# A graph layer on one core: idle lanes of a gather read rows of their own in the second pass

## The chip, the core and the metric

The kernel runs on one core of one Trainium2 chip. The metric is the device time of one execution in microseconds; lower is better. The engines are PE (TensorE), DVE (VectorE), ACT (ScalarE), POOL (GpSimd) and SP (SyncE). SP's transfers go through queue q1 of the profile, POOL's gathers through queue q0.

## The reference

One graph layer over N = 8192 nodes with F = 256 features. The adjacency is dense in memory (8192 x 8192 floats) and sparse in content, with a weight that falls off as the inverse root of the row's number, so that early rows have many edges and late rows two on average.

```
h = relu(layernorm(x))
e = leaky_relu(h @ a[:F] + (h @ a[F:]).T, 0.2)
U = softmax(where(adj > 0, e, -9e15), axis=1)
rowsum = sum(0.5 * U * U, axis=1);  coe = sigmoid(temp)
prop_u = U @ h;  xi = h * rowsum
feat = shrink(coe[2] * (prop_u - xi) + (1 - coe[2]) * (h + prop_u - xi), 1e-6)
pu = U @ feat
odd = coe[0] * (feat - coe[3] * pu) + (1 - coe[0]) * h0
even = pu + (feat - coe[3] * pu) * rowsum
out = x + coe[1] * even + (1 - coe[1]) * odd
```

## The kernel before

The rows are cut into 64 tiles of 128; a row of a tile is a lane, one of the 128 partitions. The **first pass** streams the adjacency once, finds each row's edges, and keeps for tile t and lane p up to 16 column numbers (`IDX`), their softmax weights (`WGT`) and a tail (`JT`, `ROWE`, `WE`): once no more than 128 edges of a tile are left over, each of the 128 lanes of one last gather fetches one of them, and a small matrix sends it to its row. From these it makes `feat`, kept in HBM as `feat_d`, one row of 1 KB per node.

The **second pass** computes `U @ feat` for tiles 1 to 63. Tile t has D slots and a tail; slot k is one indirect DMA (`gather_slots`, L629 to L646) in which lane p fetches row `IDX[p, t, k]` of `feat_d`; the tail is one more (`gather_tail`, L648). Each fetches 128 rows. A lane that has no edge in a slot is idle: its number in the list is OUT = 2N = 16384. In the first pass the gathers have a bounds check and an idle lane fetches nothing. In the second pass there is none; there the list is first cut to N - 1 = 8191, so all idle lanes of a gather fetch the last row of `feat_d`. Its weight is zero, so the value doesn't matter.

PE multiplies each gathered tile by a diagonal matrix of weights (`DG`, made by ACT at L680) and sums in PSUM: `first_products` (L686) and `other_products` (L691), one `If` per slot, since D differs by tile. Tile 0 has been done densely; its blocks come through `pt_d` (L1688).

Buffers form a ring of RING = 4 tiles, and each engine runs its own loop over tiles with semaphores between:

- DVE: `stage(t)` waits until tile t-4 has been multiplied (`prod2_ready`), copies tile t's lists out of the large arrays into the ring slot (`RWR`, `IDR`, `IDT`, `WSR`; L1734 to L1737) and signals `staged`. Then `finish(t-3)` makes the output rows: L1744, L1745, a wait for the product, and L1752, which signals `out_made`.
- POOL: waits for `staged`, loads the number of slots, issues the slots' gathers and the tail's. For tiles 1 to 3 part of the gathers is issued ahead, at the end of the first pass (L903, with bounds check; the rest at L1661).
- SP: loads x, h0, feat and the block of `pt_d` of tile t (L1599 to L1602) once `out_made` of tile t-4 is there, and stores the output of tile t-3 (L1609).
- ACT: waits for `staged` and for the product of two tiles before, makes the diagonals.
- PE: waits for SP's loads, the diagonals, the gathers of the tile and `out_made` of tile t-2.

`Steps` (L253 and on) chains DVE instructions where one reads what the one before wrote: each signals a semaphore and the next waits for it.

Of the kernel before, what the change touches and what calls it, by code (L numbers as in the profile page):

```python
# [7 lines left out]
ALU = mybir.AluOpType  # L8
# [4 lines left out]
def adj_preln_kernel(nc, x, adj, h0, a, temp, out):  # L13
# [39 lines left out]
    with ctx:  # L53
# [132 lines left out]
        IDT = sb("IDT", [P, RING], i32)  # L186
        IDR = sb("IDR", [P, RING, KR], i32)
        WSR = sb("WSR", [P, RING, KR])
        M24 = sb("M24", [P, K])
        U = sb("U", [P, KR])  # L190
        JNKW = sb("JNKW", [P, K])
# [160 lines left out]
        def prepare_gpsimd(pool):  # L352
            nc.gpsimd.memset(zeros[:], 0.0)
            nc.gpsimd.memset(H[:, :, :, F + 2:AUG], 0.0).then_inc(tri_set, 1)
            nc.gpsimd.memset(R[:, HO + NH * GT * AUG:], 0.0)
            nc.gpsimd.memset(ONES_K[:], 1.0)
            nc.gpsimd.memset(SLOTW[:], 1.0)
            nc.gpsimd.memset(ABOVE[:], -2.0 ** -27)
            nc.gpsimd.iota(KB[:, 0], pattern=[[1, FW]], base=-FW // 2, channel_multiplier=0, allow_small_or_imprecise_dtypes=True)
            nc.gpsimd.memset(ONE_R[:], 1.0)  # L360
            nc.gpsimd.memset(ONESB[:], 1.0)
            nc.gpsimd.memset(ZB[:], 0.0)
            nc.gpsimd.memset(TRI[:], 1.0)
            nc.gpsimd.iota(IOTAE[:], pattern=[[1, P]], base=0, channel_multiplier=0, allow_small_or_imprecise_dtypes=True)
            nc.gpsimd.iota(IOTA1[:], pattern=[[1, P]], base=1, channel_multiplier=0, allow_small_or_imprecise_dtypes=True)
            nc.gpsimd.memset(kcc[:], 0.0)
            nc.gpsimd.memset(DOWN[:], -BIG)
            nc.gpsimd.memset(FLG[:, 0:1], 0.0)
            nc.gpsimd.memset(CTL[:, 0], 1)
            nc.gpsimd.memset(JT[:, 0:1], 0)  # L370
            nc.gpsimd.memset(ROWE[:, 0:1], 0.0)
            nc.gpsimd.memset(WE[:, 0:1], 0.0)
            nc.gpsimd.iota(NEGD[:], pattern=[[-1, KC]], base=1, channel_multiplier=0, allow_small_or_imprecise_dtypes=True)
            nc.gpsimd.iota(PIDX[:], pattern=[[0, 1]], base=0, channel_multiplier=1, allow_small_or_imprecise_dtypes=True)
            nc.gpsimd.iota(ED[:, K:K + 1], pattern=[[0, 1]], base=1, channel_multiplier=1, allow_small_or_imprecise_dtypes=True)
            nc.gpsimd.memset(PLACE[:], 0.0)
            for b in range(NB):
                nc.gpsimd.memset(DROP[:, b * FW // P:(b + 1) * FW // P], -2.0 ** (b + 1))
            nc.gpsimd.iota(OFFS[:].rearrange("one (g s) -> one g s", s=FW // P), pattern=[[0, NT * P // FW], [-P, FW // P]], base=FW - P, channel_multiplier=0).then_inc(tri_set, 1)
            pool.wait_ge(tri_set, 2)  # L380
            nc.gpsimd.memset(NEGD[:, 0:1], 2.0 ** 20)
            nc.gpsimd.memset(SLOTW[:, 0:1], 0.0)
            late = SLOTW[:, KP2 + 1:KC - 1].rearrange("p (a b) -> p a b", b=2)
            nc.gpsimd.memset(late[:, :, 0], 2.0)
            nc.gpsimd.memset(late[:, :, 1], 0.0)
            nc.gpsimd.memset(SLOTW[:, KC - 1:KC], float(2 - KC))
            nc.gpsimd.affine_select(out=TRI[:], in_=TRI[:], compare_op=ALU.is_gt, fill=0.0, base=0,
                                    pattern=[[1, P]], channel_multiplier=-1)
            nc.gpsimd.iota(back[:], pattern=[[-1, NT]], base=NT, channel_multiplier=0, allow_small_or_imprecise_dtypes=True)
            nc.gpsimd.memset(ident[:], 0.0).then_inc(ident_made, 1)  # L390
            pool.wait_ge(ident_made, 1)
            nc.gpsimd.affine_select(out=ident[:], in_=ident[:], compare_op=ALU.not_equal, fill=1.0, base=0,
                                    pattern=[[-1, P]], channel_multiplier=1).then_inc(ident_made, 1)
            for g in range(NG):
                u = g % NH
                pool.wait_ge(h_done[u], g // NH + 1)
                pool.dma_start(haug_g[g], H[:, u]).then_inc(h_stored[u], 16)
            for u in range(NH):
                pool.wait_ge(h_stored[u], 16 * uses(u))
# [1174 lines left out]
        diag2_ready = sem("diag2_ready")  # L1574
        prod2_ready = sem("prod2_ready")
        s4_step = sem("s4_step")
        out_made = sem("out_made")
        out_kept = [sem(f"out_kept{v}") for v in range(RING)]
        S0A, S1A = SELF, SELF2
# [141 lines left out]
        def second_vector(dve):  # L1721
            def coefs():
                step = Steps(dve, s4_step, 0, 5)
                nc.vector.memset(SW[:, 0:1], 0.0)
                step(nc.vector.tensor_scalar(S0A[:], ROWS[:], coe[:, 1:2], one_c0[:, 0:1], ALU.mult, ALU.add))
                step(nc.vector.tensor_scalar(S1A[:], S0A[:], coe[:, 3:4], -1.0, ALU.mult, ALU.mult))
                step(nc.vector.scalar_tensor_tensor(S1A[:], S1A[:], coe[:, 1:2], INVZ[:], ALU.add, ALU.mult))
                step(nc.vector.tensor_tensor(SW[:], S1A[:], SW[:], ALU.mult))
                step(nc.vector.tensor_tensor(S0A[:], S0A[:], SW[:], ALU.add))
                step.end()  # L1730

            def stage(t, v):
                dve.wait_ge(prod2_ready, t - 3 + RING)
                nc.vector.tensor_scalar(RWR[:, v], IOTA1[:], ROWE[:, bass.ds(t, 1)], WE[:, bass.ds(t, 1)], ALU.is_equal, ALU.mult)  # L1734
                nc.vector.tensor_scalar(IDR[:, v], IDX[:, bass.ds(t, 1)].rearrange("p a k -> p (a k)"), float(N - 1), None, ALU.min)
                nc.vector.tensor_scalar(IDT[:, v:v + 1], JT[:, bass.ds(t, 1)], float(N - 1), None, ALU.min)
                nc.vector.tensor_copy(WSR[:, v], WGT[:, bass.ds(t, 1)].rearrange("p a k -> p (a k)")).then_inc(staged, 1)  # L1737

            def finish(t, r, v):
                step = Steps(dve, s4_step, t * 2 + 5, 2)  # L1740
                first = isinstance(t, int) and t == 0
                part = TD if first else TR[:, v % 2]
                dve.wait_ge(t2_loaded[v], 64 * r + 64)
                step(nc.vector.scalar_tensor_tensor(part, FR[:, v], S0A[:, bass.ds(t, 1)], XR[:, v], ALU.mult, ALU.add))  # L1744
                step.mark(nc.vector.scalar_tensor_tensor(part, H0R[:, v], one_c0[:, 1:2], part, ALU.mult, ALU.add))  # L1745
                at_least(dve, out_kept[v], 16 * r)
                dve.wait_ge(prod2_ready, t + 1 + RING)
                step.need()
                if first:
                    dve.sem_inc(out_made, 1)  # L1750
                else:
                    nc.vector.scalar_tensor_tensor(OR[:, v], ACCS[v % 2], S1A[:, bass.ds(t, 1)], TR[:, v % 2], ALU.mult, ALU.add).then_inc(out_made, 1)  # L1752
                step.end()

            def body(t, r, v, live):
                if live(0):
                    stage(t, v)
                if isinstance(t, int) and t == 1:
                    coefs()
                if isinstance(t, int) and t == 3:  # L1760
                    each_dense(dve, dense)
                if live(3):
                    finish(*ring_earlier(t, r, v, 3))
            def dense(n):
                d = tile_of(dve, n)
                step = Steps(dve, e_step, n * 7, 7)
                nc.vector.tensor_copy(dsm[:, 3:4], INVZ[:, bass.ds(d, 1)])
                step(nc.vector.tensor_copy(dsm[:, 6:7], ROWS[:, bass.ds(d, 1)]))
                dve.wait_ge(own_loaded, 48 * n + 48)
                dve.wait_ge(acc2_ready, n + 1)  # L1770
                last = out_steps(step, ACC2, XD, FD, H0D, dsm[:, 3:4], dsm[:, 6:7], dsm[:, 8:10], T0[:], OD)
                last.then_inc(out_ready, 1)
                dve.wait_ge(out_ready, n + 1)
                dve.sem_inc(acc2_free, 1)
                step.end()
            dve.sem_inc(acc2_free, 1)
            dve.wait_ge(feat_made, NS)
            dve.sem_inc(out_made, RING)
            ring_turns(dve, body, 1, 3)
            dve.wait_ge(acc0_ready, 2)  # L1780
            nc.vector.scalar_tensor_tensor(OD0, ACC3, S1A[:, 0:1], TD, ALU.mult, ALU.add).then_inc(row0_made, 1)
# [56 lines left out]
```

## Time and profile before

| | us |
|---|---|
| median of 3 runs | 1517.84 |
| lowest, highest | 1516.83, 1520.83 |
| span of the profiled execution | 1535.4 |
| POOL busy in it | 589.9 (38%) |
| DVE busy | 931.9 (61%) |
| ACT busy | 863.7 (56%) |
| PE busy | 968.4 (63%) |

The profiled execution's only time is its span, 1535.4 us from the first to the last instruction; it is 17.6 us over the median of the unprofiled runs. The page draws the span in 40 slices of 38.4 us. The first pass fills slices 1 to 26: the DMA row stands at 9 and the rate at 350 to 390 GB/s. From slice 27 on (about 1000 us) the DMA row stands at 2 to 6, POOL at 5 and 6, DVE at 1 to 3. The loop of the second pass begins at about 1080 us, where the first gather of line 1661 stands.

### The profile page before, as it was taken

The page shows a single profiled execution, that of the slowest core. Times are in us where ns is not written, and L with a number is a line of the kernel's source. Part 1 is how long each engine was busy: PE and PEld are TensorE (multiplying, and loading weights), DVE is VectorE, ACT ScalarE, POOL GpSimd, SP SyncE. Part 2 cuts the span into 40 slices and gives each one's busy share as a digit, 9 for nine tenths or more (in the row PEclk, how much of TensorE's full clock was granted, in tenths as well). Part 3 has the DMA queues.
Part 4 walks back from the last instruction along what each step waited for, and adds up shares of the span by engine and source line. Part 5 has one row for each costly group of instructions (what it writes and reads, how often), then busy time and mean ns, then how long its engine had stood idle before and what let it go on. Part 6 is the DMA issues. An engine that isn't in the chain of part 4 may idle for free.

```text
span 1535.4 us, 27679 instructions
## 1 busy us (share of the span) xinstructions
PE 968.4 (63%) x3566; PEld 578.1 (38%) x3630; DVE 931.9 (61%) x5233; ACT 863.7 (56%) x1840; POOL 589.9 (38%) x649
## 2 busy tenths in 40 slices
PE   3545767776676767667777777753464564555656
PEld 3421345443333344334343333332343343333333
DVE  7756656667778788888888888875211122223333
ACT  4663777777788888888888888831221111111111
POOL 1004344443332233322222222245656565556553
PEclk9975687889899898897878788865677676767777
DMA  7989878889899999999999999822545455556665
GB/s 190 357 292 353 322 291 300 326 327 346 330 360 369 377 368 371 361 378 394 371 385 374 372 374 376 327 62 65 150 122 145 127 161 163 158 168 180 184 184 164
DMA packets 152837, 423.14 MB, mean 276 GB/s; under 512 B 31111, under 2 KB 114697, under 8 KB 136406
## 3 DMA queue, kind: packets, MB, share of 16 engines
q1 hardware_dynamic: 122492, 345.66, 61.0%
q0 software_dynamic: 30304, 77.05, 16.7%
q8 instruction: 11, 0.18, 0.0%
q14 instruction: 30, 0.25, 0.0%
HBM read 398.37 MB, written 33.90 MB: 282 GB/s over the span
## 4 chain that ended last, share of the span: by engine, by line
DVE 31%; issue 26%; PE 15%; SPq 11%; another core or an unknown queue 6%; ACT 4%; DMA 3%; DVEq 3%; ACTq 1%
PE TP L321 5%; PE ACC L693 2%; SPq L1599 2%; SPq L1609 2%; SPq L1602 2%; DVE XHO L1066 2%; PE ACC L689 2%; SPq L1601 2%; SPq L1600 2%; PE MISC L987 2%; DMA R<-in_x_dram 1%; ACT SG L309 1%; DVEq L257 1%; DVE JK L1133 1%
## 5 line engine op out<-in xcount | busy, mean ns | idle before, releaser
L309 ACT ACTIVATE SG<-W,ABOVE 128x4096 bf16<-128x4096 f32 x126 | 467.0, 3706 | 81.0 <-DVE cnt L1049 54.3
L634 POOL DMA_INDIRECT R<-haug_d,IDS x230 | 231.0, 1004 | 604.6 <-issue 591.1
L321 PE MATMUL TP<-SG,FOLD 128*128 128x512 bf16 x948 | 299.9, 458 | 4.4 <-issue 0.7
L680 ACT ACTIVATE DG<-ident,WSR 128x128 f32<-128x128 f32 x230 | 76.6, 392 | 373.5 <-remote 234.4
L1752 DVE SCALAR_TENSOR_TENSOR R<-ACC,SELF,R 128x256 f32<-128x256 f32 x63 | 30.5, 484 | 321.6 <-remote 238.3
L634 POOL DMA_INDIRECT W<-feat_d,IDR x140 | 133.9, 956 | 117.9 <-issue 117.9
L321 PEld LDWEIGHTS TP<-SG,FOLD 128*128 128x128 bf16 x1008 | 116.9, 125 | 118.8 <-issue 62.0
L689 PE MATMUL ACC<-R,DG 128*128 128x256 f32 x446 | 158.2, 502 | 2.8 <-issue 2.7
L688 PE MATMUL ACC<-XHO,ZB 128*128 128x256 bf16 x126 | 40.1, 318 | 179.6 <-ACTq L682 86.6
L689 PEld LDWEIGHTS ACC<-R,DG 128*128 128x128 f32 x446 | 100.3, 242 | 23.4 <-issue 6.8
L689 PE MATMUL ACC<-W,DG 128*128 128x256 f32 x274 | 98.9, 503 | 11.9 <-issue 11.9
L680 ACT ACTIVATE DG<-ident,WS 128x128 f32<-128x128 f32 x230 | 75.6, 391 | 29.8 <-issue 29.8
L688 PEld LDWEIGHTS ACC<-XHO,ZB 128*128 128x128 bf16 x126 | 12.6, 100 | 210.8 <-issue 132.5
L1688 PE MATMUL MISC<-R 128*128 128x256 f32 x128 | 51.6, 493 | 52.6 <-DMA R<-pt_d 40.8
L649 POOL DMA_INDIRECT R<-haug_d,IDT x63 | 63.0, 1001 | 37.7 <-issue 37.7
L689 PEld LDWEIGHTS ACC<-W,DG 128*128 128x128 f32 x274 | 61.9, 247 | 29.3 <-issue 19.4
L634 POOL DMA_INDIRECT R<-feat_d,IDR x52 | 49.7, 955 | 41.8 <-issue 41.8
L982 PE MATMUL MISC<-RC,ONESB 128*128 128x18 bf16 x61 | 11.7, 191 | 84.6 <-DVE RC L1181 84.4
L950 PE MATMUL OWNB<-HTS,R 128*128 128x256 f32 x116 | 39.4, 421 | 36.9 <-issue 19.6
L1688 PEld LDWEIGHTS MISC<-R 128*128 128x128 f32 x128 | 28.5, 242 | 69.0 <-DMA R<-pt_d 43.2
L803 ACT ACTIVATE WS<-SCR,msm 128x25 f32<-128x25 f32 x63 | 19.9, 316 | 60.6 <-DVE msm L1108 44.7
L649 POOL DMA_INDIRECT W<-feat_d,IDT x48 | 46.2, 962 | 16.3 <-issue 16.0
(295 smaller groups left out, 2292.7 us busy)
## 6 DMA issues: line engine op xcount, KB each, us to landing
W<-in_adj_dram SPq DMA_DIRECT2D x128, 2048.0 KB, 13.6
haug_d<-R POOLq DMA_DIRECT2D x8, 1056.0 KB, 9.7
HTS<-haug_d SPq DMA_DIRECT2D x64, 132.0 KB
R<-in_x_dram SPq DMA_DIRECT2D x8, 1024.0 KB, 6.6
R<-in_x_dram SPq DMA_DIRECT2D x64, 128.0 KB
R<-in_L_gnn_h_dram SPq DMA_DIRECT2D x64, 128.0 KB
R<-feat_d SPq DMA_DIRECT2D x64, 128.0 KB
out_dram<-R SPq DMA_DIRECT2D x64, 128.0 KB, 1.8
```

Of the source, the lines that this page charges most:

```text
L309: nc.scalar.activation(SG[:, u, half(h)], W2[:, u, half(h)], ACT.Sign, scale=2.0 ** 100, bias=ABOVE[:], accum_out=DEG[:, u, h:h + 1]).then ...
L321: nc.tensor.matmul(KP[u], FOLD[:, b], SG[:, u, b * FW:(b + 1) * FW], start=False, stop=False)
L634: pool.indirect_dma_start(out=g[:, k, 0:w], out_offset=None, in_=table, in_offset=bass.IndirectOffsetOnAxis(ap=ids[:, k:k + 1], axis=0), * ...
L649: pool.indirect_dma_start(out=g[:, KR, 0:w], out_offset=None, in_=table, in_offset=bass.IndirectOffsetOnAxis(ap=idt, axis=0), **limit).the ...
L680: nc.scalar.mul(DG[:, u, k], ident[:], weights[:, k:k + 1])
L688: nc.tensor.matmul(ACCS[u], ZB[:], COLS[:, 0:F], start=True, stop=False)
L689: first_slots(pe, slots, lambda k: nc.tensor.matmul(ACCS[u], DG[:, u, k], g[:, k, 0:F], start=False, stop=False))
L693: other_slots(pe, slots, lambda k: nc.tensor.matmul(ACCS[u], DG[:, u, k], g[:, k, 0:F], start=False, stop=False))
L950: nc.tensor.matmul(ACC0, PTB[:, w], HTS[:, uc, 0:F], start=False, stop=False)
L987: nc.tensor.matmul(SPR, RE[:, u], ED[:], start=True, stop=True).then_inc(spread, 1)
L1066: swap(KB[:, 0], FOUND[:, 0:8], KP[u], EMPTY).then_inc(keys_taken[u], 1)
L1688: own = nc.tensor.matmul(ACC3, PTR[:, v], FR[:, v], start=False, stop=False)
```

## The change

The change touches the second pass alone, but for one table that POOL writes in the prologue. An idle lane no longer gets the number N - 1, but one of its own: `AWAY[p, k] = 64 p + 3 k - OUT` is added to the list wherever it holds OUT, so that lane p reads row 64 p + 3 k in slot k (k = 16 for the tail). Rows have 1 KB: the lanes' idle rows lie 64 KB apart, the slots' 3 KB. All of them lie under row 8192.

```diff
+        AWAY = sb("AWAY", [P, KS1])
+        IDLE = sb("IDLE", [P, RING, KS1])
...
+            nc.gpsimd.iota(AWAY[:], pattern=[[3, KS1]], base=int(-OUT), channel_multiplier=N // P, allow_small_or_imprecise_dtypes=True)
...
+        idle_step = sem("idle_step")
...
             def stage(t, v):
                 dve.wait_ge(prod2_ready, t - 3 + RING)
                 nc.vector.tensor_scalar(RWR[:, v], IOTA1[:], ROWE[:, bass.ds(t, 1)], WE[:, bass.ds(t, 1)], ALU.is_equal, ALU.mult)
-                nc.vector.tensor_scalar(IDR[:, v], IDX[:, bass.ds(t, 1)].rearrange("p a k -> p (a k)"), float(N - 1), None, ALU.min)
-                nc.vector.tensor_scalar(IDT[:, v:v + 1], JT[:, bass.ds(t, 1)], float(N - 1), None, ALU.min)
+                step = Steps(dve, idle_step, t, 1)
+                ids = IDX[:, bass.ds(t, 1)].rearrange("p a k -> p (a k)")
+                nc.vector.scalar_tensor_tensor(IDLE[:, v, 0:KR], ids, float(N - 1), AWAY[:, 0:KR], ALU.is_gt, ALU.mult)
+                step(nc.vector.tensor_scalar(IDLE[:, v, KR:KS1], JT[:, bass.ds(t, 1)], float(N - 1), AWAY[:, KR:KS1], ALU.is_gt, ALU.mult))
+                step.end()
+                nc.vector.tensor_tensor(IDR[:, v], ids, IDLE[:, v, 0:KR], ALU.add)
+                nc.vector.tensor_tensor(IDT[:, v:v + 1], JT[:, bass.ds(t, 1)], IDLE[:, v, KR:KS1], ALU.add)
                 nc.vector.tensor_copy(WSR[:, v], WGT[:, bass.ds(t, 1)].rearrange("p a k -> p (a k)")).then_inc(staged, 1)
```

DVE's own order, one turn of the loop from the staging of a tile to the output before the next. Before (WI is the array that holds `IDX` and `WGT`, R the one with the ring's buffers):

```order
L1734 TENSOR_SCALAR R<-IOTA,ROWE,WE 128x128
L1735 ISA
L1735 TENSOR_SCALAR IDR<-WI 128x16
L1736 REGISTER_ALU
L1736 TENSOR_SCALAR IDT<-JT 128x1
L1737 ISA
L1737 COPY WSR<-WI 128x16
L1744 ISA
L1744 SCALAR_TENSOR_TENSOR R<-R,SELF 128x256
```

With the change, where L1753 is what was L1744:

```order
L1738 TENSOR_SCALAR R<-IOTA,ROWE,WE 128x128
L1741 ISA
L1741 SCALAR_TENSOR_TENSOR IDLE<-WI,AWAY 128x16
L1742 REGISTER_ALU
L1742 TENSOR_SCALAR IDLE<-JT,AWAY 128x1
L1744 TENSOR_TENSOR IDR<-WI,IDLE 128x16
L1745 TENSOR_TENSOR IDT<-JT,IDLE 128x1
L1746 ISA
L1746 COPY WSR<-WI 128x16
L1753 ISA
L1753 SCALAR_TENSOR_TENSOR R<-R,SELF 128x256
```

Two DVE instructions and one wait have come in ahead of the copy to `WSR`, which signals `staged`; the order of the rest, and of the gathers on POOL, is as it was.

## Rows read from the trace of the kernel before

**Rows 1.** Windows of the second pass: busy us of each engine, clock, DMA share, GB/s.

```profile
core 0: us, PE busy (x) PEld busy (x) DVE busy (x) ACT busy (x) POOL busy (x), PEclk, DMA share, GB/s
1100.00:1150.00 50.00, 27.77 (x93) 20.38 (x92) 7.59 (x28) 10.26 (x33) 28.42 (x31) 0.69 0.43 118
...
1450.00:1500.00 50.00, 27.50 (x82) 16.65 (x82) 17.88 (x68) 6.75 (x20) 25.97 (x28) 0.77 0.64 182
```

**Rows 2.** POOL's groups by line, 1030 us to the end.

```profile
L634 POOL DMA_INDIRECT W<-feat_d,IDR x140 | 133.9, 956 | 117.9 <-issue 117.9
L634 POOL DMA_INDIRECT R<-feat_d,IDR x52 | 49.7, 955 | 41.8 <-issue 41.8
L649 POOL DMA_INDIRECT W<-feat_d,IDT x48 | 46.2, 962 | 16.3 <-issue 16.0 <-DVE WSR L1737 0.3
```

**Rows 3.** POOL's timeline: four gathers, a long gap, the next two.

```profile
1246.18 0.95 POOL L634 DMA_INDIRECT W<-feat_d,IDR  x1 [0.31 <-issue]
1247.43 0.95 POOL L649 DMA_INDIRECT W<-feat_d,IDT  x1 [0.30 <-issue]
1254.29 0.95 POOL L634 DMA_INDIRECT W<-feat_d,IDR  x1 [5.91 <-issue]
1255.54 1.05 POOL L634 DMA_INDIRECT W<-feat_d,IDR  x1 [0.31 <-issue]
```

**Rows 4.** POOL's timeline: first and last of the 28 gaps over 0.6 us.

```profile
1121.18 0.95 POOL L634 DMA_INDIRECT W<-feat_d,IDR  x1 [7.26 <-issue]
...
1517.79 0.95 POOL L634 DMA_INDIRECT W<-feat_d,IDR  x1 [1.43 <-issue]
```

**Rows 5.** DVE's timeline inside the gap of rows 3.

```profile
1251.91 0.48 DVE L1752 SCALAR_TENSOR_TENSOR R<-ACC,SELF,R 128x256 f32<-128x256 f32 x1 [16.89 <-remote]
1252.31 0.34 DVE L1734 TENSOR_SCALAR R<-IOTA,ROWE,WE 128x128 f32<-128x128 f32 x1
1252.56 0.17 DVE L1735 TENSOR_SCALAR IDR<-WI 128x16 int32 x1
1252.64 0.14 DVE L1736 TENSOR_SCALAR IDT<-JT 128x1 int32 x1
1252.71 0.16 DVE L1737 COPY WSR<-WI 128x16 f32 x1
1252.78 0.48 DVE L1744 SCALAR_TENSOR_TENSOR R<-R,SELF 128x256 f32<-128x256 f32 x1
1253.29 0.48 DVE L1745 SCALAR_TENSOR_TENSOR R<-R,one_c 128x256 f32<-128x256 f32 x1
1253.90 0.48 DVE L1752 SCALAR_TENSOR_TENSOR R<-ACC,SELF,R 128x256 f32<-128x256 f32 x1
```

**Rows 6.** Chain of waits that ended last, 1244 to 1254.5 us: start, us, what.

```profile
1246.60 0.70 issue
1247.30 0.69 SPq L1599
1247.98 0.73 issue
...
1250.12 0.69 SPq L1599
1250.81 0.70 issue
1251.51 0.01 SPq L1600
```

**Rows 7.** PE's timeline around the same gap.

```profile
1246.66 1.19 PE L693 MATMUL ACC<-W,DG 128*128 128x256 f32 x2 [0.20 <-issue]
1251.59 1.22 PE L694 MATMUL ACC<-W,R 128*128 128x256 f32 x2 [3.74 <-issue]
```

**Rows 8.** DMA queues, window 200 to 400 us: packets, MB, share of 16 engines.

```profile
q0 software_dynamic: 4080, 9.09, 12.8%
```

**Rows 9.** DMA queues, window 1051 to 1068 us.

```profile
q0 software_dynamic: 624, 1.24, 25.1%
```

**Rows 10.** DMA queues, window 1100 to 1200 us.

```profile
q0 software_dynamic: 3001, 8.18, 31.1%
```

**Rows 11.** DMA queues, window 1400 to 1500 us.

```profile
q0 software_dynamic: 2738, 7.48, 29.0%
```

**Rows 12.** POOL's timeline 1055 to 1058 us, and the chain beside it.

```profile
1055.14 1.00 POOL L903 DMA_INDIRECT W<-feat_d,WI  x1 [0.30 <-issue]
1056.45 1.00 POOL L903 DMA_INDIRECT W<-feat_d,WI  x1 [0.31 <-issue]
```

**Rows 13.** Chain of waits that ended last, 1054 to 1062 us.

```profile
1055.24 0.27 DVE lkey L1241 x2
...
1055.88 1.44 DVE lkey L1241 x2
```

**Rows 14.** Timelines of DVE and POOL around another gap's end.

```profile
1314.22 0.16 DVE L1737 COPY WSR<-WI 128x16 f32 x1
...
1315.81 0.95 POOL L634 DMA_INDIRECT W<-feat_d,IDR  x1 [3.58 <-issue]
```

**Rows 15.** Timelines of POOL and DVE in the prologue.

```profile
3.80 0.15 POOL L373 IOTA NEGD<- 128x18 f32 x1
...
6.61 0.29 POOL L392 TENSOR_SCALAR_AFFINE_SELECT ident<-ident 128x128 f32<-128x128 f32 x1
...
10.11 2.25 DVE L507 TENSOR_SCALAR FOLD<-ident 128x128 bf16<-128x128 f32 x16
```

## The prediction

> **What bounds the kernel now.** The change lies in the second pass, so I read the 40 slices of the page first, to see where that pass begins (the DMA row drops from 9), then the windows of its stretches. In [rows 1] no engine is full: of 50 us POOL is busy 28 and 26, DVE 8 and 18, PE 28, and the DMA engines stand at 0.43 and 0.64. So neither bytes nor arithmetic bind; something waits in turn. POOL's groups say how [rows 2]: a gather takes 0.956 us whatever it fetches, and 0.30 us passes before the next, so 1.25 us apiece. The page counts 140 + 52 + 48 + 15 gathers of the loop and 12 of line 1661, 267 in all; 267 x 1.25 = 334 us of the pass. The rest of POOL's time is gaps. POOL's timeline shows them [rows 3, 4]: runs of gathers 1.25 us apart and then a hole. From 1085 us on there are 28 holes over 0.6 us; 21 of them are 2.9 to 7.3 us long, and together the 28 make 111 us. The pass is therefore POOL's issue (334 us) plus these holes (111 us), and a change that makes no gather fewer can act on the holes alone.
>
> How does a hole end? Take that of [rows 3], from 1248.38 to 1254.29. On PE, a product of the tile that POOL waits for starts only at 1251.59, 3.74 us after the one before [rows 7]; DVE's L1752 follows at 1251.91, then the staging, whose last instruction ends at 1252.71 + 0.16 = 1252.87 [rows 5]; POOL starts 1.42 us later. What holds PE is neither a semaphore nor a transfer that the profile names. In the chain of waits the sequencers' small steps (register moves, branches, DMA issues) take 0.69 to 0.73 us each while gathers are in flight, and 0.01 us from 1251.5 on, after the last gather has drained [rows 6]. So the rhythm is: POOL issues for about four tiles, everybody else crawls, the ring of four runs dry, POOL stops, the others recover at full speed, DVE stages, POOL starts again.
>
> **The change part by part.**
>
> *What idle lanes cost today.* I counted them from the reference's adjacency by the kernel's rule for slots: for tiles 4 to 63 there are 252 gathers (the same number as in the trace) with 7189 idle lanes of 32256, 22%; some 15% in the early tiles, about 30% in the last third. If reading one row from many lanes were slow, q0's time per MB should be higher than where idle lanes fetch nothing, and should grow with the idle share. The queue rows give share x 16 engines x window / MB. In the first pass, idle lanes skipped, it is 0.128 x 16 x 200 / 9.09 = 45 ns per KB [rows 8]; in the gathers issued ahead, also skipped, 0.251 x 16 x 17 / 1.24 = 55 [rows 9]; in the second pass 0.311 x 1600 / 8.18 = 61 early [rows 10] and 0.290 x 1600 / 7.48 = 62 late [rows 11]. The idle share doubles from the third to the fourth, and the price rises by 2%. The nearest row to the second pass is that of rows 9 (same table, same 1 KB rows, gathers in a long run), so I bound the gain in q0's time at (61 - 55) / 61 = 10%, and from below at zero. The 45 of the first pass is the far bound (25%), kept for a rival. What hangs on it: after POOL's last issue the gathers need until about 1250.2 to drain (the 0.7 us steps stop one step later, [rows 6]), 1.8 us. Ten per cent of that is 0.18 us in each of 28 holes, 5 us at most; half of the bound, 2.5 us, enters the sum. Between holes a faster packet buys nothing, since POOL paces them at 1.25 us.
>
> *The crawl.* Might it come from the hot row? It is there as well beside gathers of line 903 [rows 12], whose idle lanes are skipped: the same pair of DVE instructions that takes 0.27 us takes 1.44 us there, with a step of 0.7 us twice in it [rows 13]. So I expect the crawl to stay.
>
> *Staging.* Removed: L1735 (0.17 us) and L1736 (0.14) [rows 5]. Added: a SCALAR_TENSOR_TENSOR and a TENSOR_TENSOR on 128x16, a TENSOR_SCALAR and a TENSOR_TENSOR on 128x1, and one wait on DVE's own semaphore. Today the chain runs from 1252.31 to 1252.87, 0.56 us: L1735 starts 0.25 after L1734, L1736 and L1737 0.07 to 0.08 after each other. With the change: the first of the new starts at +0.25, the second at +0.33 and ends at +0.48; the wait holds the next until it has ended, and such a dependent start stands 0.03 us after its predecessor's end at L1744 to L1745 and 0.13 after it at L1745 to L1752 [rows 5]; then +0.07, +0.07 and 0.16 for the copy. That ends at 0.81 to 0.91 instead of 0.56: 0.25 to 0.35 us later, and I take 0.30. Behind the wait on DVE stand the copy to WSR, so `staged`, so POOL's gathers and ACT's diagonals, and the finish of the tile three back. Where a run of gathers goes on, tile t was staged long before POOL comes to it, and the 0.30 us is hidden behind the 4 to 5 us of gathers per tile. At a hole nothing hides it: POOL restarts 1.42 us after the copy's end here and 1.43 us after it in another hole [rows 14]. 28 x 0.30 = 8.4 us.
>
> *POOL beside DVE.* Three of the added instructions read two tiles of SBUF. The gather at 1255.54, beside L1745 which does so too, took 1.05 us instead of 0.95 [rows 3, 5]; over all gathers the mean is 956 ns against 950 [rows 2], that is 267 x 0.006 = 1.6 us for some 60 us of L1744 and L1745. The new ones add about half that work: +1 us. The Trainium skill, in "SBUF — State Buffer" on the port pair shared by DVE and GpSimd, says that a DVE instruction with two SBUF inputs and a GpSimd operation that reads SBUF exclude each other for a whole instruction; that rule speaks against the change, and the 0.10 us agrees in sign, but by the mean it bites rarely.
>
> *The rest.* One table more from POOL in the prologue: a table of 18 columns takes 0.15 us there, POOL is done with its prologue at 6.9 us and DVE takes up `ident` at 10.1 us [rows 15], so 3 us of other work hide it. Gathers, bytes and their number: unchanged.
>
> *Paid back.* During a hole the other engines run some ten times faster than in the crawl, so a hole that is 0.3 us longer lets PE and SP get ahead, and the next hole may be shorter. That is certain neither way: full return would make the staging free, none would cost 8.4. Of the 21 long holes I take half of 21 x 0.3 = 6.3 back, 3.1 us.
>
> **Sum.** +8.4 + 1 - 2.5 - 3.1 = +3.8 us. Against the profiled execution 1535.4 becomes 1539; the same difference on the median of the runs, 1517.8, gives 1522.
>
> **The rivals.**
>
> *Staging on the path of every recovered tile (slower).* In a hole two tiles are finished in a row, 1251.91 and 1253.90, 1.99 us apart, and between them DVE runs nearly without rest [rows 5]: DVE itself paces the recovery, PE waits for `out_made`. If each such turn grows by 0.3 us and nothing is paid back, two per hole cost 28 x 2 x 0.3 = 17 us: 1535. It decides if the second L1752 of a recovery comes 2.3 us after the first and PE stands waiting for it.
>
> *The hole's length is set by work, not by delays (no change).* If the ring needs a certain amount of full-speed time per tile, POOL's later restart only fills time that was needed: 1518. For it: the holes vary from 0.7 to 7.3 us with the same chain at their end.
>
> *The last row is a hot spot (faster).* Then q0's time falls toward the first pass's 45 ns per KB, 25%, and the crawl with it; 25% of 111 us of holes less the 9 us of staging is 19 us: 1499; with half of that effect, 1509. Against it: the flat 61 and 62 of [rows 10, 11] and the crawl beside skipped lanes. It pays from a fall of q0's time by about 10%.
>
> *The new rows collide instead.* They lie 64 KB apart by lane. The Trainium skill, "DMA: Bandwidth & Descriptors", in its table of latencies and other measured facts, says that row pitches at large powers of two (512 KiB and up) cost up to half of the rate. No row of this case has such a pitch, 64 KB is below the page's range, and both the old and the new choice could fall under it; the sum stays as it is. Without the page: 22% of the lanes can hardly add more than 10% to q0's time, 5 us in the holes, so 1527.
>
> That the change doesn't do what it says I can exclude from the code: every idle entry is exactly OUT, and 64 x 127 + 48 = 8176 is a row of the table.
>
> **How the numbers follow.** About 0.3% (4.6 us) is what a measurement of this kernel can tell from no change: faster is below 1513.3, slower above 1522.4. Forecast, 1519 to 1526, chance 0.42, of which 0.24 falls within 0.3% and 0.18 slower. Every-tile staging, 1529 to 1537, 0.17: slower. Work-set holes, 1516 to 1520, 0.20: same. Hot spot, 1497 to 1513, 0.15: faster. Colliding rows, 1524 to 1530, 0.04: slower. Something else, 0.02. That makes faster 0.16, same 0.45, slower 0.39. The range 1508 to 1534 leaves out the better half of the hot spot and the end of the every-tile case.
>
> **What the profile after would show.** Right: L1746's copy ends 0.8 to 0.9 us after L1738 starts, POOL restarts 1.4 us behind it, about 28 holes with a sum of 110 to 120 us, q0 at 58 to 62 ns per KB, sequencer steps of 0.7 us during runs. Wrong: q0 under 55 ns per KB, holes under 100 us in sum, or runs of gathers clearly longer than four tiles would mean that idle reads did hold up the others; turns of 2.3 us in the recoveries with more than 125 us of holes would mean the first rival.

## The result, and the profile after

The changed kernel takes 1522.7 us (median of 20 runs, 1519.3 to 1527.1); the kernel before, run beside it, takes 1518.4 (median of 20, 1509.4 to 1524.7). The ratio of the two is 1.0034, with a 95% interval of 1.0021 to 1.0047: slower by 4.3 us, a little more than the 0.3% that was named as what can be told from no change. The interval reaches from 0.2% to 0.5%, so the size is known to a factor of two.

The two profiled executions don't show this sign. That of before spans 1535.4 us and lies 17 us over its median, that of after spans 1517.9 and lies 5 us under its own. Single executions of one kernel differ by more than the change is worth; the median and the ratio say what it costs, and the profiles say how. The profile of before is an odd one besides: the first gather of its loop starts at 1081.2 us, in all thirteen others of this document between 1066.9 and 1072.2, so some 11 of the 17 us were lost before the loop. Its windows lie 9 to 14 us earlier in the work than those of the others, and sums over its loop need a second trace beside them.

The page of the changed kernel has in its part on busy time:

```profile
PE 971.0 (64%) x3629; PEld 576.9 (38%) x3630; DVE 955.0 (63%) x5361; ACT 863.1 (57%) x1840; POOL 588.8 (39%) x650
```

DVE has 23 us more than before (931.9) and POOL the same. Windows of 100 us in the second pass; [rows 1] has windows of 50 us out of the same two stretches (columns as there):

```profile
1100.00:1200.00 100.00, 54.89 (x176) 38.70 (x175) 19.71 (x81) 20.07 (x62) 56.76 (x60) 0.70 0.44 129
...
1400.00:1500.00 100.00, 64.24 (x175) 36.87 (x175) 43.08 (x173) 13.46 (x39) 54.57 (x58) 0.76 0.66 194
```

POOL is busy 57 and 55 of 100 us with some 60 gathers in each stretch, 28 and 26 of 50 before, and the clock granted to TensorE stands at 0.70 and 0.76 where it stood at 0.69 and 0.77. POOL's groups from 1030 us on, which answer to [rows 2]:

```profile
L637 POOL DMA_INDIRECT W<-feat_d,IDR x140 | 134.0, 957 | 119.9 <-issue 119.9
L637 POOL DMA_INDIRECT R<-feat_d,IDR x52 | 49.8, 957 | 33.4 <-issue 33.4
L652 POOL DMA_INDIRECT W<-feat_d,IDT x48 | 45.8, 953 | 16.3 <-issue 16.3
```

A gather takes 957, 957 and 953 ns, before 956, 955 and 962: the added DVE work takes nothing from POOL's gathers. There are 28 gaps over 0.6 us in the loop, as before, with a sum of 106 us against 111; in a second execution of the same kernel it is 26 and 110. The 111 is that of the odd profile: four kernels below whose staging is no longer than before's have 98 to 103 us (own rows alone 102, all lanes on own rows 98, the added steps in `finish` 103, the row table late 100).

A hole's end, first on POOL, then on DVE, to be laid beside [rows 3] and [rows 5]:

```profile
1246.69 0.95 POOL L652 DMA_INDIRECT W<-feat_d,IDT  x1 [0.30 <-issue]
1253.29 0.95 POOL L637 DMA_INDIRECT W<-feat_d,IDR  x1 [5.66 <-issue]
1254.54 1.17 POOL L637 DMA_INDIRECT W<-feat_d,IDR  x1 [0.30 <-issue]
```

```profile
1250.34 0.48 DVE L1761 SCALAR_TENSOR_TENSOR R<-ACC,SELF,R 128x256 f32<-128x256 f32 x1 [15.50 <-remote]
1250.73 0.34 DVE L1738 TENSOR_SCALAR R<-IOTA,ROWE,WE 128x128 f32<-128x128 f32 x1
1250.99 0.17 DVE L1741 SCALAR_TENSOR_TENSOR IDLE<-WI,AWAY 128x16 f32<-128x16 f32 x1
1251.07 0.21 DVE L1742 TENSOR_SCALAR IDLE<-JT,AWAY 128x1 f32 x1
1251.32 0.18 DVE L1744 TENSOR_TENSOR IDR<-WI,IDLE 128x16 int32<-128x16 f32 x1
1251.41 0.15 DVE L1745 TENSOR_TENSOR IDT<-JT,IDLE 128x1 int32<-128x1 f32 x1
1251.48 0.17 DVE L1746 COPY WSR<-WI 128x16 f32 x1
1251.66 0.48 DVE L1753 SCALAR_TENSOR_TENSOR R<-R,SELF 128x256 f32<-128x256 f32 x1
1252.18 0.48 DVE L1754 SCALAR_TENSOR_TENSOR R<-R,one_c 128x256 f32<-128x256 f32 x1
1252.80 0.49 DVE L1761 SCALAR_TENSOR_TENSOR R<-ACC,SELF,R 128x256 f32<-128x256 f32 x1
```

From the start of L1738 to the end of the copy it is 1251.65 - 1250.73 = 0.92 us, before 0.56. The two output rows stand 1252.80 - 1250.34 = 2.46 us apart, before 1.99. From the start of the output row to POOL's first gather it is 2.95 us here, in [rows 3, 5] 1254.29 - 1251.91 = 2.38. I took that last span in every gap over 2 us of both traces. Before, 14 of 21 have 2.38 to 2.41. After, nine of 20 have 2.73 to 2.75 and nine 2.95 to 3.01; seven of the second group are the holes in which POOL starts 1.64 us after the copy and not 1.43. Without the longest in each (4.2 and 17 us) the means are 2.46 and 2.88: 0.4 us later per long hole.

q0's queue in the windows of [rows 10] and [rows 11], 1100 to 1200 us and 1400 to 1500 us (packets, MB, share of 16 engines):

```profile
q0 software_dynamic: 2928, 8.00, 28.2%
...
q0 software_dynamic: 2792, 7.61, 28.1%
```

That is 0.282 x 1600 / 8.00 = 56 ns per KB and 59, before 61 and 62: 7 and 5% less. Over the longer stretch from 1100 to 1450 us it is 58 against 60, 4% less. Own rows are cheaper to fetch, and the kernel is slower all the same.

### The profile page after: what moved, and what is told of

The parts are those of the page before. It is cut to its first block, busy times and chain, and to the rows that moved or that the text cites. A ratio compares the mean times of both kernels' runs of the same rounds, so it can differ in the third digit from the quotient of the medians.

```text
span 1517.9 us, 27871 instructions
## 1 busy us (share of the span) xinstructions
PE 971.0 (64%) x3629; PEld 576.9 (38%) x3630; DVE 955.0 (63%) x5361; ACT 863.1 (57%) x1840; POOL 588.8 (39%) x650
## 4 chain that ended last, share of the span: by engine, by line
DVE 31%; issue 27%; PE 15%; SPq 7%; DMA 6%; another core or an unknown queue 5%; ACT 4%; DVEq 3%; ACTq 2%; POOL 0%; POOLq 0%
PE ACC L692 4%; PE TP L323 3%; PE ACC L696 3%; DVE XHO L1069 2%; SPq L1606 2%; PE MISC L990 2%; DMA R<-sc_d 2%; DMA R<-in_x_dram 1%; SPq L1604 1%; SPq L1603 1%; SPq L1605 1%; SPq L1613 1%; ACT SG L311 1%; DVE RE L1201 1%
## 5 line engine op out<-in xcount | busy, mean ns | idle before, releaser
L323 PE MATMUL TP<-SG,FOLD 128*128 128x512 bf16 x1008 | 306.7, 447 | 0.0
L1761 DVE SCALAR_TENSOR_TENSOR R<-ACC,SELF,R 128x256 f32<-128x256 f32 x63 | 30.5, 484 | 289.8 <-remote 173.2
```

Of the source, the lines that this page charges most:

```text
L323: nc.tensor.matmul(KP[u], FOLD[:, b], SG[:, u, b * FW:(b + 1) * FW], start=False, stop=False)
```

## The experiments

Each ratio is to the kernel before on the same chip, with its 95% interval.

**The change once more** gives the comparison for what follows.

> The change as it is, again, beside its parts on the same chip. All theories: 1.003 (+4 us), as measured before. In one profile of it: staging (L1738 to the end of L1746) 0.92 us against 0.56.

Measured: 1522.1 us, ratio 1.0039 (1.0017 to 1.0061). The cost is there again.

**The longer staging alone.** The change with the old row: the table holds the same number for every lane.

```diff
-            nc.gpsimd.iota(AWAY[:], pattern=[[3, KS1]], base=int(-OUT), channel_multiplier=N // P, allow_small_or_imprecise_dtypes=True)
+            nc.gpsimd.memset(AWAY[:], float(N - 1) - OUT)
```

> The new staging with the old rows: AWAY holds N - 1 - OUT everywhere, so idle lanes read the last row again. Theory 1 (the longer staging costs, the rows give a little back): +4 to +8 us against before, no faster than the change. Theory 2 (the staging is free and the new rows, 64 KB apart, cost): 0 us. Queue q0 by theory 1: 61 ns per KB in the windows of the second pass, where the change has 56 to 59.

Measured: 1519.2 us, ratio 1.0027 (1.0006 to 1.0049). A loss is here without a single row changed; by the middle value it is most of that of the change, by the interval anything from 1 to 7 us.

**The own rows alone.** Staging as before; the lists of tiles 4 to 63 are rewritten once, by four instructions, when DVE is at tile 3.

```diff
...
+            def spread_lists():
+                step = Steps(dve, idle_step, 0, 1)
...
+                nc.vector.scalar_tensor_tensor(IDLE[:, RING:], ids, float(N - 1), away, ALU.is_gt, ALU.mult)
+                step(nc.vector.tensor_scalar(IDLT[:], jt, float(N - 1), AWAY[:, KR:KS1], ALU.is_gt, ALU.mult))
+                nc.vector.tensor_tensor(ids, ids, IDLE[:, RING:], ALU.add)
+                nc.vector.tensor_tensor(jt, jt, IDLT[:], ALU.add)
+                step.end()
```

> The new rows with the old staging: the lists of tiles 4 to 63 are rewritten once, ahead of the loop's steady part (about 2.5 us of DVE), and the staging per tile is that of before. Tiles 1 to 3 still read the last row. Theory 1: 0 to -4 us against before (the rows give 0 to 5 us, the one rewriting takes up to 2.5). Theory 2: +4 us.

Measured: 1515.4 us, ratio 1.0000 (0.9979 to 1.0021). The rewriting itself could have hidden a gain; DVE's timeline of this kernel says that it didn't:

```profile
1070.79 1.15 DVE L1748 SCALAR_TENSOR_TENSOR IDLE<-WI,AWAY 128x960 f32<-128x960 int32 x1
...
1073.21 0.21 DVE L1751 TENSOR_TENSOR JT<-JT,IDLT 128x60 int32<-128x60 int32 x1
...
1107.23 0.48 DVE L1767 SCALAR_TENSOR_TENSOR R<-ACC,SELF,R 128x256 f32<-128x256 f32 x1 [29.98 <-remote]
```

It takes 2.6 us, and soon after it DVE stands still for 30 us. q0 between 1100 and 1450 us, first with own rows alone, then with the longer staging alone:

```profile
q0 software_dynamic: 10224, 27.93, 29.0%
```

```profile
q0 software_dynamic: 10285, 28.11, 30.2%
```

By the same working, share x 16 x 350 / MB, that is 58 and 60 ns per KB. So the faster fetch is real, 4%, and buys no time that shows; the interval of own rows alone is 3 us to either side. The staging costs by both comparisons: the change with its own rows is 6.7 us over own rows alone (1522.1 and 1515.4, same chip), the longer staging alone 3.5 us over the kernel before. By these runs the change is the sum of its halves within their noise.

**A staging longer by three more steps.** Three dependent steps of 0.2 us that multiply `IDLE` by one.

```diff
-                step = Steps(dve, idle_step, t, 1)
+                step = Steps(dve, idle_step, t * 4, 4)
...
+                for _ in range(3):
+                    step(nc.vector.tensor_scalar(IDLE[:, v], IDLE[:, v], 1.0, None, ALU.mult))
```

> The change with three more dependent steps on the small IDLE tile in each staging (multiply by 1), each with its wait: the staging grows by about 0.6 us more. Theory 1, holes counted one by one with half paid back: +0.6 x 28 x 0.6 = +10 us on top of the change, +14 in all. If every recovered tile pays: +20 or more on top. Theory 3 (holes set by work, restart delays are paid back in full): no more than the change, +4 us.

Measured: 1524.7 us, ratio 1.0054 (1.0033 to 1.0076). DVE's timeline at a hole's end of this kernel, whose POOL starts again at 1200.80:

```profile
1197.42 0.48 DVE L1763 SCALAR_TENSOR_TENSOR R<-ACC,SELF,R 128x256 f32<-128x256 f32 x1 [16.68 <-remote]
1197.83 0.34 DVE L1738 TENSOR_SCALAR R<-IOTA,ROWE,WE 128x128 f32<-128x128 f32 x1
...
1198.40 0.60 DVE L1744 TENSOR_SCALAR IDLE<-IDLE 128x17 f32<-128x17 f32 x3
...
1199.20 0.17 DVE L1748 COPY WSR<-WI 128x16 f32 x1
...
1200.44 0.48 DVE L1763 SCALAR_TENSOR_TENSOR R<-ACC,SELF,R 128x256 f32<-128x256 f32 x1
```

Staging now lasts 1199.37 - 1197.83 = 1.54 us, 0.98 more than before, and the output rows are 3.02 us apart. 28 holes would pay 28 x 0.98 = 27 us if nothing came back, and 28 x 2 x 0.98 = 55 if every recovered tile paid; the kernel pays 8, by its interval 5 to 12, where theory 1 had 14. Some 60 to 80% comes back. That is the strongest evidence against the first rival: a turn that is a whole microsecond longer ought to have cost tens of microseconds. Against the change it is only 2.6 us more, and the two intervals overlap, so that the last 0.62 us of staging cost anything isn't shown.

**Is the last row slow when everybody reads it?** All lanes of the loop's gathers read row 8191. This leaves out the neighbours' rows and with them the product of the second pass; its time is what counts.

```diff
-                nc.vector.tensor_scalar(IDR[:, v], IDX[:, bass.ds(t, 1)].rearrange("p a k -> p (a k)"), float(N - 1), None, ALU.min)
+                nc.vector.tensor_scalar(IDR[:, v], IDX[:, bass.ds(t, 1)].rearrange("p a k -> p (a k)"), float(N - 1), float(N - 1), ALU.min, ALU.max)
...
```

The tail's list `IDT` is changed in the same way, here and in the next kernel.

> Staging as before, but every lane of every gather of the second pass's loop reads the last row (the neighbours' rows are left out). Theory 1 (a row read by many lanes costs little): q0 rises from 60.5 ns per KB in proportion to the lanes that share the row, 22% to 100%, about 2.3 x 4.5 = 10 to 70 to 72, and the time by 0 to 8 us. Theory of the hot spot: q0 over 80 ns per KB and the time up by 20 us and more.

Measured: 1621.6 us, ratio 1.0673 (1.0645 to 1.0702), 104 us slower. **And do rows 64 KB apart collide?** All lanes read row 64 p + 3 k instead, again without the neighbours' rows; staging has its old length.

```diff
-                nc.vector.tensor_scalar(IDR[:, v], IDX[:, bass.ds(t, 1)].rearrange("p a k -> p (a k)"), float(N - 1), None, ALU.min)
+                nc.vector.tensor_scalar(IDR[:, v], AWAY[:, 0:KR], float(N - 1), None, ALU.min)
...
```

> Staging as before, but every lane of every gather of the loop reads row 64 p + 3 k (the neighbours' rows are left out): rows 64 KB apart by lane, for all lanes. If that pitch collides, q0 is above the 60.5 ns per KB of before and the time is up. Theory 1: 50 to 58 ns per KB, time -5 to 0 us against before.

Measured: 1514.6 us, ratio 0.9974 (0.9953 to 0.9994). q0 between 1100 and 1450 us, all lanes on the last row, then all on rows of their own:

```profile
q0 software_dynamic: 8430, 23.04, 70.9%
```

```profile
q0 software_dynamic: 10286, 28.08, 28.6%
```

The first is 0.709 x 5600 / 23.04 = 172 ns per KB, far over the 80 named for the hot spot, the second 57. So a row that is read by all is a hot spot, by a factor of three: a gather of 128 KB then needs 128 x 172 / 16 = 1.38 us of all 16 engines, more than the 1.25 us at which POOL issues, and the transfers take over as the bound. The DMA engines are busy at 0.93 between 1100 and 1200 us where before they stood at 0.45 (columns as in [rows 1]), and POOL's holes grow from 7.3 us at most to 17:

```profile
1100.00:1200.00 100.00, 39.92 (x118) 29.05 (x118) 11.70 (x42) 15.14 (x47) 43.73 (x46) 0.65 0.93 105
```

```profile
1184.14 0.95 POOL L634 DMA_INDIRECT W<-feat_d,IDR  x1 [17.25 <-issue]
...
1204.96 0.95 POOL L634 DMA_INDIRECT W<-feat_d,IDR  x1 [13.59 <-issue]
```

But it is far from linear. With 22% of the lanes on the row, 57 + 0.22 x (172 - 57) = 82 ns per KB would follow; the rows show 60. Rows 64 KB apart are the cheapest of all, so they don't collide. This kernel gains 0.26%, at most 0.5% by its interval, with rows of their own for all 128 lanes; for the 22% that the change spreads, the run with own rows alone has found nothing.

**Idle lanes that fetch nothing.** The lists keep OUT, and the second pass's gathers get the bounds check that the first pass has.

```diff
-                    gather_slots(pool, t, RINGS[v], IDR[:, v], feat_d, F, gathered2[v])
-                gather_tail(pool, RINGS[v], IDT[:, v:v + 1], feat_d, F, gathered2[v])
+                    gather_slots(pool, t, RINGS[v], IDR[:, v], feat_d, F, gathered2[v], bounds_check=N - 1, oob_is_err=False)
+                gather_tail(pool, RINGS[v], IDT[:, v:v + 1], feat_d, F, gathered2[v], bounds_check=N - 1, oob_is_err=False)
...
-                nc.vector.tensor_scalar(IDR[:, v], IDX[:, bass.ds(t, 1)].rearrange("p a k -> p (a k)"), float(N - 1), None, ALU.min)
+                nc.vector.tensor_scalar(IDR[:, v], IDX[:, bass.ds(t, 1)].rearrange("p a k -> p (a k)"), OUT, None, ALU.min)
...
```

The gathers of line 1661 get the check too, and `IDT` the same limit as `IDR`.

> Idle lanes fetch nothing: the lists keep OUT and the gathers of the second pass have the bounds check of the first. Theory 1: POOL's gather with a check takes 1.00 us where one without takes 0.955 (L634 in the first pass, mean 1004 ns), 267 of them make +12 us on POOL; 22% fewer bytes on q0 give at most 5 us in the holes: +6 to +12 us. If idle reads were what holds the others up, the holes would shrink by 20 us and more: -10 us.

Measured: 1502.9 us, ratio 0.9898 (0.9875 to 0.9921). I had expected it to be slower, because POOL's gather grows and POOL's issue is three quarters of the loop. It is 1% faster. So the next question was which half of the edit does it.

**The bounds check alone.** The check of the diff above, with `IDR` and `IDT` cut to N - 1 as before: idle lanes still read the last row, so that nothing is ever out of bounds and no byte is saved.

> The bounds check on the gathers of the second pass, but idle lanes still read the last row, so that nothing is skipped: only POOL's price of the check. POOL's gather 1.00 us instead of 0.956. If all of it shows, 267 x 0.05 = +13 us; then the skipped bytes themselves were worth 28 us in the run that skipped. If the holes take it up: 0 to +5 us, and the skipped bytes were worth 15 to 20.

Measured: 1500.2 us, ratio 0.9903 (0.9876 to 0.9930), the same as with skipping within some 5 us. POOL's groups from 1030 us on, with the bounds check alone:

```profile
L634 POOL DMA_INDIRECT W<-feat_d,IDR x140 | 140.8, 1006 | 86.8 <-issue 86.5 <-DVE WSR L1738 0.3
L634 POOL DMA_INDIRECT R<-feat_d,IDR x52 | 52.3, 1006 | 32.7 <-issue 28.1 <-DVE WSR L1738 4.6
```

and with skipping:

```profile
L634 POOL DMA_INDIRECT W<-feat_d,IDR x140 | 141.0, 1007 | 83.4 <-issue 83.1 <-DVE WSR L1738 0.3
```

A gather takes 1006 ns where it took 956 [rows 2], so POOL issues 1.31 us apart and loses 267 x 0.05 = 13 us. The idle time ahead of the first group falls from 117.9 to 86.8 us, and all gaps over 0.6 us of the loop together from 111 to 78. Against the odd profile of before that is too much: beside the 98 to 103 us of the four kernels named above it is 20 to 25 us less. From the first gather of the loop to the end of the last it is 418 us here and 416 with skipping, 427 to 433 in those four, 440 in before's profile. POOL's timeline of the kernel with the check alone has this:

```profile
1201.17 0.99 POOL L634 DMA_INDIRECT W<-feat_d,IDR  x1 [0.30 <-issue]
1202.47 1.23 POOL L634 DMA_INDIRECT W<-feat_d,IDR  x1 [0.30 <-DVE WSR L1738]
1204.00 0.99 POOL L649 DMA_INDIRECT W<-feat_d,IDT  x1 [0.30 <-issue]
...
1210.51 0.99 POOL L634 DMA_INDIRECT W<-feat_d,IDR  x1 [0.30 <-issue]
1212.32 0.99 POOL L649 DMA_INDIRECT W<-feat_d,IDT  x1 [0.81 <-issue]
1217.90 1.22 POOL L634 DMA_INDIRECT R<-feat_d,IDR  x1 [4.59 <-DVE WSR L1738]
```

The gathers of a run stand mostly 1.30 us apart, and at 1202.47 a gather is released by DVE's staging with no hole ahead of it. Why a slower gather makes the pass shorter isn't settled by this. It may be the pace, which leaves the other sequencers 5% more time per gather. Or it may be what the check changes in how the gather is put together: in the traces of both kernels POOL's sequencer has one register move (`MOVE` of lines 634, 649 and 1661) ahead of each gather, 266 in the loop, where before has one in all. The crawl has not gone. Counting register moves, loads, branches and DMA issues that last over 0.5 us between the first and the last gather, the four engines other than POOL have 284 with the check alone, 324 with skipping, and 328 to 399 in the kernels without the check (399 before); the last kernel of this section, which has the check too, has 349, so the fall isn't a clear one. On POOL itself such slow steps rise, from 56 before to 131 and 124, on the moves among others. A plain pause of 0.05 us on POOL would tell the two apart; it wasn't tried. What is shown is that the bytes don't matter much: 22% fewer of them on q0 bring nothing beyond the check that shows within some 5 us.

**Getting the added steps off the path.** First the new `IDLE` instructions ahead of stage's own wait.

```diff
-                dve.wait_ge(prod2_ready, t - 3 + RING)
-                nc.vector.tensor_scalar(RWR[:, v], IOTA1[:], ROWE[:, bass.ds(t, 1)], WE[:, bass.ds(t, 1)], ALU.is_equal, ALU.mult)
...
+                dve.wait_ge(prod2_ready, t - 3 + RING)
+                nc.vector.tensor_scalar(RWR[:, v], IOTA1[:], ROWE[:, bass.ds(t, 1)], WE[:, bass.ds(t, 1)], ALU.is_equal, ALU.mult)
```

> The change with its two IDLE instructions and their wait moved ahead of the wait for the product of tile t - 4, so that DVE does them while it would wait, and RWR, IDR, IDT and WSR follow the wait. Theory 1 (what costs is the length of the chain from the product to the signal): staging after the wait 0.56 us as before, and the time falls back by 3 to 5 us, to 0 to +2 us against before. If DVE's added work itself costs: as the change, +5 us.

Measured: 1521.8 us, ratio 1.0025 (1.0005 to 1.0045). The move took nothing off the path, as DVE's timeline at a hole's end shows:

```profile
1197.42 0.48 DVE L1761 SCALAR_TENSOR_TENSOR R<-ACC,SELF,R 128x256 f32<-128x256 f32 x1 [17.36 <-PE ACC L697]
1197.82 0.17 DVE L1739 SCALAR_TENSOR_TENSOR IDLE<-WI,AWAY 128x16 f32<-128x16 f32 x1
1197.90 0.21 DVE L1740 TENSOR_SCALAR IDLE<-JT,AWAY 128x1 f32 x1
1198.26 0.35 DVE L1743 TENSOR_SCALAR R<-IOTA,ROWE,WE 128x128 f32<-128x128 f32 x1 [0.15 <-DVE IDLE L1740]
...
1198.68 0.17 DVE L1746 COPY WSR<-WI 128x16 f32 x1
```

The product that `stage` waits for has been waited for already by the `finish` just before it. The long wait stands ahead of L1761, not in `stage`, and the new instructions are still between L1761 and the signal: 1198.85 - 1197.42 = 1.43 us, a little more than the change's 1251.65 - 1250.34 = 1.31. So this run tests nothing about the chain.

So in the next kernel they went into the `finish` before, ahead of its wait for the product.

```diff
-            def finish(t, r, v):
+            def finish(t, r, v, following):
...
+                if following:
+                    idle_rows(*following)
```

> The change with the two IDLE instructions of tile t moved into the finish before, ahead of its wait for the product, so that they are done before L1752 of the tile that ends a hole (in the version with only the own wait behind them they still stood between that L1752 and the signal, since the same product had been waited for before it). From L1752 to the end of the copy 0.97 us as before, not 1.31. Theory 1 (what costs is the chain from product to signal): back to -1 to +1 us against before. If DVE's added work or POOL's sharing of a port costs: +3 to +6 us, as the change.

Measured: 1518.2 us, ratio 1.0021 (1.0006 to 1.0036). DVE's timeline, whose POOL starts again at 1195.14:

```profile
1192.73 0.48 DVE L1769 SCALAR_TENSOR_TENSOR R<-ACC,SELF,R 128x256 f32<-128x256 f32 x1 [16.04 <-remote]
1193.13 0.34 DVE L1745 TENSOR_SCALAR R<-IOTA,ROWE,WE 128x128 f32<-128x128 f32 x1
1193.38 0.17 DVE L1750 TENSOR_TENSOR IDR<-WI,IDLE 128x16 int32<-128x16 f32 x1
...
1193.54 0.17 DVE L1752 COPY WSR<-WI 128x16 f32 x1
...
1194.53 0.17 DVE L1740 SCALAR_TENSOR_TENSOR IDLE<-WI,AWAY 128x16 f32<-128x16 f32 x1
1194.62 0.21 DVE L1741 TENSOR_SCALAR IDLE<-JT,AWAY 128x1 f32 x1
1194.75 0.48 DVE L1769 SCALAR_TENSOR_TENSOR R<-ACC,SELF,R 128x256 f32<-128x256 f32 x1
```

The chain is that of before again: 1193.71 - 1193.13 = 0.58 us of staging, 1195.14 - 1192.73 = 2.41 to POOL's restart, 2.02 between output rows. The new instructions lie where DVE would wait. Still 0.2% stays. The interval excludes zero narrowly and overlaps that of the change, so this run can't say how much of the cost the chain carried; it does say that a chain of the old length didn't bring all of it back. What else the added instructions cost is open.

**A chain shorter than before's.** The kernel before with the row table's instruction behind the signal, on a semaphore of its own for which PE waits.

```diff
-                nc.vector.tensor_scalar(RWR[:, v], IOTA1[:], ROWE[:, bass.ds(t, 1)], WE[:, bass.ds(t, 1)], ALU.is_equal, ALU.mult)
...
+                nc.vector.tensor_scalar(RWR[:, v], IOTA1[:], ROWE[:, bass.ds(t, 1)], WE[:, bass.ds(t, 1)], ALU.is_equal, ALU.mult).then_inc(rows_staged, 1)
```

> The kernel before with RWR (0.34 us, 0.25 of them in the chain) made behind the copy that signals staged, under a semaphore of its own for PE. The chain from L1752 to the signal is 0.25 us shorter than before. Theory 1, by the slope measured with the staging 0.36 us longer (+4 to +6 us) and 1.06 us longer (+8): -2 to -3 us. If the holes' length were set by work alone: 0.

Measured: 1515.4 us, ratio 1.0003 (0.9986 to 1.0020), with 2.14 us from the output row to POOL's restart instead of 2.39. A chain 0.25 us shorter should give 28 x 0.25 = 7 us, or 3 after the same share is paid back. It gives nothing that shows: by the interval between 2 us gained and 3 lost, so that 7 us are excluded and 3 just so. The same edit on top of the skipping:

> Idle lanes skipped by the bounds check, and RWR behind the signal: both parts that shorten holes. -15 us for the first as measured, -2 us more for the second: 1500 to 1503 us, ratio 0.988.

Measured: 1504.0 us, ratio 0.9920 (0.9891 to 0.9949); no better than skipping alone, 0.9898.

The fastest versions are that with the check alone, 1500.2 us, and that with skipping, 1502.9. Both are 1% under the kernel before and some 20 us under the changed one, and they can't be told apart.

## Why the prediction was right, and where it was not

The forecast was 1522 us, +3.8 on the sum; measured is 1522.7, +4.3. The most likely case named was within 0.3%, and the ratio lies just beyond that bound. Point by point:

**Staging, +8.4.** The time that it adds to the chain was right and a little short. I had 0.25 to 0.35 us; it is 0.36 on DVE's timeline and 0.4 to POOL's restart, since in seven of 20 holes POOL starts 1.64 us after the copy instead of 1.43. Why there are two values I can't say; with the three steps more, and with the `IDLE` instructions moved into the `finish` before, nearly all are 1.43. So the term should read 28 x 0.36 = 10 us, 28 x 0.4 = 11 at most. That the loss comes with the staging's instructions and not with the rows is shown: +0.27% with staging alone, 0.00% with rows alone, and the change 6.7 us over rows alone. That it acts by the length of the chain, as the term has it, is not: with the chain at its old length 0.2% stays, and a chain shorter by 0.25 us gains nothing.

**POOL beside DVE, +1.** Not there. The gathers' mean is 957 ns against 956. By the rule on the shared port pair, in "SBUF — State Buffer" of the Trainium skill, a DVE instruction with two SBUF inputs and a GpSimd operation that reads SBUF exclude each other. If a gather that reads its list counts as that, the added instructions should have cost something. The traces agree only for the long instructions of `finish`: all 20 gathers of before's loop that took over 1.0 us, and all 17 of after's (1.17 us at 1254.54 above is one), overlap one of the 0.48 us two-input instructions. In after's trace 29 gathers overlap an added instruction and none of `finish`'s; they took 940 to 965 ns, so the short ones cost POOL nothing.

**Own rows, -2.5.** The fetch did get cheaper, 56 and 59 ns per KB where 58 to 62 was expected, by 4% over the longer stretch where half of the 10% bound was taken. The time it was to bring, -2.5 us, doesn't show: 0.0, with an interval of about 3 us to either side, which doesn't exclude the term. Four per cent of a drain of 1.8 us in 28 holes would be 2 us, too little for these runs. The sentence that between holes a faster packet buys nothing is not contradicted.

**Paid back, -3.1.** Mis-sized. Staging's 10 us come out as 4, and the longer staging's 27 as 8: six to seven parts in ten come back, where I had half of the long holes' share. If the rows are put at nothing, the errors of the terms are +1.6 for staging, -1 for POOL, +2.5 for the rows and -2.6 for the payback, and they nearly cancel: that the sum came out within 0.5 us was in part luck.

**The rivals.** Staging on the path of every recovered tile: one of its signs showed, turns of 2.46 us instead of 1.99, but its price did not. The gaps' sum was 106 and 110 us, not over 125, and a turn of 3.02 us cost 8 us and not 55. Holes set by work: it is wrong as it was put, since a longer staging costs time, but its other direction is right: the chain cut by 0.25 us gains nothing, and one put back to its old length leaves 0.2%. My reading is that some of the rhythm is set by work, and that my model of a fixed delay per hole describes an added delay at best; no run separates this from another cost of the added instructions. The hot spot: real, and too small at 22% of the lanes; where between 22% and all lanes it begins to cost time isn't known. Colliding rows: refuted at this pitch. The Trainium skill, "DMA: Bandwidth & Descriptors", in its table of latencies and other measured facts, has the loss at row pitches of 512 KiB and up; at 64 KB the trace shows none (57 ns per KB against 60 before).

**What the argument of the first part got wrong.** "The pass is POOL's issue plus these holes" was read as if the two could be priced apart. The bounds check adds 13 us to the one and takes 20 to 25 from the other (34 against the odd profile of before), and the kernel gains 15. The pace of the gathers and the length of the holes changed together, and a price put on POOL's issue alone, as I did for the kernels with the check, has the wrong sign.

## What to carry to other kernels

Price an edit on the chain from a signal to the restart of the engine that stood still, and then expect most of it back where the other engines are catching up in that pause; two longer stagings cost about a third of their length here and a shorter chain brought nothing. A fetch that was 4% cheaper on a queue that an engine paces brought no time that could be measured, so look at what the issuing engine does per gather before looking at what idle lanes fetch. When two of a rhythm's parts add up to the whole, change one and watch the other before pricing either alone. And take a second profile of the kernel before when sums over a loop are to be compared: one execution here had 9 to 13 us more of holes than four close relatives of the same kernel.

## What the runs showed of the hardware

- A bounds check on an indirect DMA makes POOL's instruction 1006 ns instead of 956, and this kernel 1% faster (0.9903, 0.9876 to 0.9930) though it saves no byte. POOL's sequencer has one register move more per gather with it.
- One 1 KB row read by all 128 lanes of every gather costs q0 172 ns per KB against 57 for rows of their own, and the kernel 104 us; read by 22% of the lanes it costs 60 against 58, and no time that can be measured.
- Rows 64 KB apart for all lanes are no slower than the graph's own: 57 ns per KB, ratio 0.9974.
- Gathers over 1.0 us long (20 before, 17 after) all ran beside a 128x256 DVE instruction with two SBUF inputs, 0.48 us long; beside the added ones on 128x16 and 128x1, 0.15 to 0.21 us long, 29 gathers took 940 to 965 ns.
- After a hole POOL's first gather follows the staging's copy by 1.43 us in most cases and by 1.64 in seven of 20 with the change; the cause is open.
